# Expert stage: the token sum of a routed row moves from VectorE to POOL, and VectorE finishes the row's targets two steps later

## The reference

```
x = layernorm(x + self_attention(x))
x = layernorm(x + cross_attention(x, ctx))
x = layernorm(x + ffn(x))

ffn: logits = x @ gate_w.T ; the 8 best of 64 experts, their weights by a softmax
     gate, up = split(x @ gu_w[e].T)           # 64 + 64 columns
     out = sum over the 8 experts of weight[e] * ((silu(gate) * up) @ dp_w[e].T)
     out += sigmoid(x @ sh_gate1_w.T) * shared_expert(x)
```

## Time and profile before

| | us |
|---|---|
| median of 3 runs | 1711.96 (1709.74 to 1717.92) |
| the profiled execution | 1717.95 |
| its span, first to last instruction | 1716.2 |
| PE busy, share of the span | 1461.1, 85% |
| DVE busy | 1134.9, 66% |
| POOL busy | 1000.0, 58% |
| ACT busy | 770.8, 45% |
| mean granted TensorE clock | 0.939 |

### The profile page before, as it was taken

One profiled execution on the slowest core, in us unless ns is written; L12 is line 12 of the kernel. 1 busy time (PEld: TensorE's weight loads), 2 busy tenths in 40 slices (PEclk: granted clock), 3 DMA queues, 4 the chain that ended last, 5 costly groups with the idle time before them and its releaser, 6 DMA issues. The chain is left out here.

```text
span 1716.2 us, 35026 instructions
## 1 busy us (share of the span) xinstructions
PE 1461.1 (85%) x9324; PEld 1183.5 (69%) x9324; DVE 1134.9 (66%) x3731; ACT 770.8 (45%) x2649; POOL 1000.0 (58%) x991
## 2 busy tenths in 40 slices
PE   3799999999999999999998727877877787887587
PEld 2688888888888888888887625655655555665464
DVE  2568787878778888888887444455555555344398
ACT  2465656565565565555655112322322232232254
POOL 3446777776766776777766424455555555555322
PEclk8799999999999999999999759899899999889799
DMA  7333232323232212122212946656656556554697
GB/s 259 101 119 104 98 117 83 125 78 119 86 111 75 83 58 80 64 74 66 72 64 83 291 150 186 185 173 174 188 168 186 171 170 177 173 172 134 228 417 318
DMA packets 184341, 247.99 MB, mean 144 GB/s; under 512 B 30796, under 2 KB 160921, under 8 KB 179748
## 3 DMA queue, kind: packets, MB, share of 16 engines
q1 hardware_dynamic: 150820, 171.55, 32.7%
q0 software_dynamic: 27648, 69.28, 11.0%
q10 hardware_dynamic: 5760, 5.87, 1.0%
HBM read 136.98 MB, written 117.98 MB: 149 GB/s over the span
## 5 line engine op out<-in xcount | busy, mean ns | idle before, releaser
L1623 POOL DMA_INDIRECT expert_out_scratch<-y,targets x320 | 318.9, 997 | 277.2 <-DVE targets L1832 104.8
L573 POOL DMA_INDIRECT slot_scratch<-xrow x256 | 273.6, 1069 | 194.4 <-issue 90.4
L1682 PE MATMUL bank_g<-gu,x_turned 128*128 (+1 forms) x1408 | 213.6, 299 | 29.8 <-issue 18.8
L1682 PEld LDWEIGHTS bank_g<-gu,x_turned 128*128 128x128 f32 x1408 | 189.2, 209 | 48.7 <-issue 47.8
L1840 DVE TENSOR_TENSOR inter<-silu,bank_g 128x128 f32<-128x128 f32 x176 | 50.3, 286 | 256.9 <-ACT silu L1748 213.4
L1741 ACT ACTIVATE x_turned<-bank_x 128x512 f32<-128x512 f32 x176 | 105.4, 599 | 231.2 <-PE bank_x L1664 144.7
L860 ACT ACTIVATE q_work<-q_work 128x128 f32<-128x128 f32 x512 | 151.1, 298 | 128.9 <-DVE q_work L1058 110.3
L764 PE MATMUL bank_d<-wo_w,o2t 128*128 128x256 f32 x1536 | 194.5, 287 | 3.0 <-DVE o2t L977 3.0
L764 PEld LDWEIGHTS bank_d<-wo_w,o2t 128*128 128x128 f32 x1536 | 188.7, 194 | 3.1 <-DVE o2t L977 3.1
L1701 PE MATMUL bank_y<-dp,inter_t 64*128 (+1 forms) x352 | 132.8, 460 | 49.7 <-DVE y L1849 23.1
L522 POOL TENSOR_TENSOR q_rs<-q_ve,minus_half 128x8 f32<-128x8 f32 x64 | 105.5, 1648 | 89.4 <-DVE q_ve L1048 88.8
(11 more groups left out here) (253 smaller groups left out, 3225.9 us busy)
## 6 DMA issues: line engine op xcount, KB each, us to landing
x_rows<-slot_scratch SPq DMA_DIRECT2D x320, 136.0 KB
results<-expert_out_scratch SPq DMA_DIRECT2D x32, 1024.0 KB, 8.8
slot_scratch<-zeros SPq DMA_DIRECT2D x16, 816.0 KB, 4.5
dp<-in_down SPq DMA_DIRECT2D x161, 64.0 KB
slot_scratch<-zeros SPq DMA_DIRECT2D x8, 1088.0 KB, 8.4
gu<-in_gate_up SPq DMA_DIRECT2D x11, 768.0 KB
expert_out_scratch<-y,targets POOLq DMA_INDIRECT x320
token_row_scratch<-xrow SPq DMA_DIRECT2D x32, 136.0 KB
```

The costliest lines, as they stand in the source:

```text
L573: nc.gpsimd.indirect_dma_start(out=slot_d[:, :], out_offset=bass.IndirectOffsetOnAxis(ap=xrow[slot][:, SLOT8 + k:SLOT8 + k + 1].bitcast(U3 ...
L1623: nc.gpsimd.indirect_dma_start(out=y_d[:, :], out_offset=bass.IndirectOffsetOnAxis(ap=target[n % 8][:, j:j + 1], axis=0), in_=y[s % HELD][ ...
L1682: mm = nc.tensor.matmul(bank_g[:, s % 2, j * P:(j + 1) * P], xt[s % 2][:, j, c, :], w, start=(c == 0), stop=(c == C - 1))
```

## The change

For every sparse row tile POOL adds `matched` and the token column (`sum_row`, one 128x1 addition per tile, so two per step) into a new tile `summed`. Two rows' sums (n = 0 and 1) are made before the loop. After that `scatter(s)`, behind its three waits, does for j = 0, 1: the sum of tile j of row n + 2, then the indirect DMA of tile j of row n. `matched` and `summed` have 8 places each. DVE's `name_row` is now a maximum with 0 and a minimum with 65535 on `summed`, with the conversion to integer. It runs at s - 2 in the place where it ran at s, that is before `copy_y(s-3)`, and waits for POOL's two sums of its row; `bound_row` too runs at s - 2. `match_row(s)` no longer waits for a name but for the match two rows back, and from row 8 on for POOL's sum 8 rows back. SP's `free_rows` waits for POOL's sum of the row that leaves, not for its name. `find_weights` gets one wait on its own engine's earlier result.

```diff
-        matched = [sb(f"matched{n}", [P, 2]) for n in range(2)]
+        matched = sb("matched", [P, 8, 2])
+        summed = sb("summed", [P, 8, 2])
@@ SP, free_rows
-                        sp.wait_ge(sig["row_named"], number(s - 8) + 1)
+                        sp.wait_ge(sig["row_summed"], 2 * number(s - 8) + 2)
@@ POOL
+            SUMMED_AHEAD = 2
+
+            def sum_row(n, j):
+                if n >= SPARSE_STEPS:
+                    return
+                pool.wait_ge(sig["row_matched"], 2 * n + j + 1)
+                if n >= 8:
+                    pool.wait_ge(sig["row_named"], n - 7)
+                nc.gpsimd.tensor_tensor(summed[:, n % 8, j:j + 1], matched[:, n % 8, j:j + 1],
+                                        x_in[steps_of["sparse", n] % 8][:, j, TOK:TOK + 1], ALU.add)\
+                    .then_inc(sig["row_summed"], 1)
             def scatter(s):
                 n = number(s)
                 pool.wait_ge(sig["y_copied"], s + 1)
                 pool.wait_ge(sig["row_bounded"], n + 1)
                 pool.wait_ge(sig["y_ready"], min(s + 2, STEPS))
                 for j in range(2):
+                    sum_row(n + SUMMED_AHEAD, j)
                     nc.gpsimd.indirect_dma_start(
...
+            for n in range(SUMMED_AHEAD):
+                for j in range(2):
+                    sum_row(n, j)
             for s in range(STEPS):
                 if sparse(s):
                     scatter(s)
@@ DVE, match_row
                 if n >= 2:
-                    dve.wait_ge(sig["row_named"], n - 1)
+                    dve.wait_ge(sig["row_matched"], 2 * n - 2)
+                if n >= 8:
+                    dve.wait_ge(sig["row_summed"], 2 * (n - 7))
...
             def name_row(s):
                 n = number(s)
-                dve.wait_ge(sig["row_matched"], 2 * n + 2)
-                nc.vector.tensor_tensor(named[n % 2][:, :], matched[n % 2][:, :], x_in[s % 8][:, :, TOK], ALU.add)\
+                dve.wait_ge(sig["row_summed"], 2 * (n + 1))
+                nc.vector.tensor_scalar(named[n % 2][:, :], summed[:, n % 8, :], 0.0, 65535.0, ALU.max, ALU.min)\
                     .then_inc(sig["row_named"], 1)
@@ DVE, find_weights
                 if stage == 0:
+                    dve.wait_ge(sig["w_summed"], t)
@@ DVE, order of the loop
-                if now:
-                    name_row(s)
+                named_now = s - 2 >= 0 and s - 2 < STEPS and sparse(s - 2)
+                if named_now:
+                    name_row(s - 2)
                 if 0 <= s - 3 < STEPS:
                     copy_y(s - 3)
-                if now:
-                    bound_row(s)
+                if named_now:
+                    bound_row(s - 2)
```

More of the change, by code:

```diff
@@ L1412 @@
 x_turned x_copied gate_up_done silu_done gated inner_turned inner_copied y_ready y_copied
-row_matched row_named row_bounded
+row_matched row_summed row_named row_bounded
 y_stored0 y_stored1 y_stored2 y_stored3 y_stored4 y_stored5 y_stored6 y_stored7
@@ L1815, in match_row @@
                                                    slot_of[:, 0, 2 * n + j:2 * n + j + 1], column[:, :], ALU.is_equal,
-                                                   ALU.mult, accum_out=matched[n % 2][:, j:j + 1])\
+                                                   ALU.mult, accum_out=matched[:, n % 8, j:j + 1])\
                         .then_inc(sig["row_matched"], 1)
```

## The result

The changed kernel takes 1789.32 us (median, 1782.58 to 1793.89); the kernel before, measured beside it, takes 1714.94. The medians lie 74 us apart (4.3%); the ratio on record, which isn't the one of the medians, is 1.0415, with an interval of 1.0384 to 1.0446. So the change makes the kernel about 4% slower. The forecast was 1798 (1735 to 1885). The profiled execution took 1793.89 us, its span was 1792.2 and the mean granted clock 0.934.

What follows compares the result with a forecast made beforehand. No engine was full; POOL's DMA runs and pauses set 3.31 us a step. With 130 steps at 4.11 us and 46 at 3.0, the stage gains 89 us, less 3 at the end: 1712 + 86 = 1798 us, range 1735 to 1885.

Steps and rivals of the forecast that it cites:

- the ring: Expert stage: projection, POOL's DMA and second sum, DVE's name and copy, next projection wait in a circle; floor 3.72 us.
- tight steps: Expert-stage steps whose name waits for a sum made behind the projection just finished: 130 of 176, at 4.11 us each.
- the first sum: POOL's addition ahead of a scatter's first DMA: adds between 0 and 0.13 us a turn; 0.13 taken.
- lower clock: Projection at 1.2 GHz takes 1.22 us instead of 0.70; in a quarter of the steps, adding 0.13 us a turn.
- The later wake-up: POOL's start after the projection's end: 1.00 us taken instead of 0.87, adding 0.13 us a turn.
- The relaxed steps: Expert-stage steps whose sum is made a scatter earlier: 46 of 176, between 2.23 and 3.31 us, 3.0 taken.
- The end: After the last projection: POOL's last DMA lags 2.3 us instead of 6.2; 3 us taken back.
- the beat of the stage: Expert stage before the change: four POOL DMAs, three gaps and a 2.04 us pause, 6.82 us for two steps.
- the short and the long loop: Expert-stage rivals: all at the 3.72 us floor, 1730 us, chance 0.08; pauses or dearer sums, 1851 to 1919 us, 0.22.
- the main case: Whole kernel: expert stage +89 us, 3 back at its end, 1798 us, own range 1762 to 1840; chance 0.58.
- By POOL's own throughput that costs nothing: POOL's sums in the expert stage: 2 x (1.27 + 0.13) = 2.80 us a step, under the 3.31 of before.
- 64 x 0.68 = 44 us: Sums held up by DVE's 64 two-input weight searches, up to 0.68 us each: 44 us more, 1842 us.

Runs made afterwards that it cites:

- experiment 6: Kernel before, without sums, POOL clearing a small tile between its two DMAs and the copy of y waiting for the clear of two rows earlier: 1729.03 us, 1.1098.
- experiments 1 to 4: Changed kernel with sums one scatter earlier 0.9991, both sums ahead of the first DMA 1.004, name behind copy 0.9969; kernel before plus unread POOL sums 0.9995.
- experiment 5: Changed kernel with every sum made twice, first into a tile that nobody reads: 1809.08 us, 1.1595 against the kernel before on its chip.
- experiment 3: Changed kernel with the name behind the copy of y in DVE's order: 1710.72 us, 0.9969 against the kernel before.
- experiment 9: Kernel before, unchanged, profiled on a chip of the second kind: 1560.99 us, 0.9988.
- experiment 7: Kernel before without the second indirect DMA of every scatter, the last stage reading token rows instead of experts' outputs: 1548.91 us in a single run.
- experiment 4: Kernel before, DVE still adding, naming and bounding as there, plus POOL's 320 sums into a tile that nobody reads: 1713.58 us, 0.9995.
- experiment 11: Kernel before plus POOL's 320 sums into a tile that nobody reads, on a chip of the second kind: 1603.24 us, 1.03.
- experiment 8: Changed kernel with sums made one scatter earlier and the name behind the copy, on a chip of the second kind: 1588.19 us, 1.0189.

## Why the prediction was right, by its own steps

**The mechanism** was right, and it is shown and not only argued: closing the ring without any sum loses the time (experiment 6, on a chip of the second kind), opening it at any of three places, or leaving out the wait, gives it back (experiments 1 to 4, on the first chip).

**The ring's terms**, by the medians of the tight steps of the changed kernel:

| term | forecast | measured |
|---|---|---|
| projection's end to the first DMA, with the first sum | 0.87 + 0.13 + 0.13 | 0.94 (0.94 to 1.38) |
| the DMA | 0.97 | 1.00 |
| second sum and handing over | 0.13 + 0.05 | 0.22 + 0.04 |
| name, until the copy starts | 0.07 | 0.08 |
| copy | 0.69 | 0.69 |
| copy's end to the projection's end | 0.24 + 0.70 | 0.94 |
| lower clock | 0.13 | none in the median, at most 0.08 in the mean |
| **a turn** | **4.11** | **3.92** (mean 4.02) |

- *The sum* was mis-sized: 0.206 us in the mean, not 0.13. The way I got 0.13, extrapolating two wide additions to width 1, gives over a third too little; it lay inside the bounds of 0.13 and 0.65.
- *The first sum* costs nearly nothing: POOL starts it 0.24 us after the projection's end (1107.38 - 1107.14), and there are 0.52 us of gap behind it. A DMA of an idle POOL took 0.87 us to start without a sum and 0.94 with one: most of the sum lies inside the start-up (with two sums ahead of the DMA it is 0.98, experiment 5). I had added it whole.
- *The later wake-up* of 0.13 was not needed; the mean is 0.96, with the first sum in it, and the worst 1.38.
- *The clock.* I wrote "under 0.92 in the stage", at PE 55% busy. It was 0.92 and 0.95, at 73% and 71% busy by the rows above, no lower than in the earlier trace rows. The error is in the 2.23 of 4.1: that is PE's shortest turn, but PE is busy 0.73 x 3.71 = 2.7 us a step here, and was 0.80 x 3.31 = 2.6 before. The mean of the tight steps stands 0.10 over the median: 0.08 lie between the copy's end and the projection's end, where the projection takes up to 1.22 us instead of 0.70, and 0.02 in late wake-ups.
- *The relaxed steps*: 3.0 forecast, 2.81 in the mean of 42 (median 2.49).
- *Number of steps*: by the projections' ends, without the first ten, the tight ones went from 3.20 to 4.02 us (123 of them: +101 us) and the relaxed ones from 3.69 to 2.81 (42: -37). The two together make 64 of the 70 us; the first ten make up the rest. The stage's forecast was +89 and it became +70, by terms that were nearly all a little too large.
- *The end*: I took 3 us back, it was 1.2. POOL's last DMA starts 4.7 us behind the last projection's end in the changed kernel, not 2.3: the last two rows, four DMAs and not two, are still scattered one after another behind it. (Before it was 5.95 us and not 6.2, as the last projection ran at the lower clock and took 0.63 us, not 0.38.)
- *What the sum didn't have*: the stage begins 7 us later. The start of the first projection differs by up to 17 us among the profiled kernels (1019.2 in experiment 6, 1036.2 in experiment 3), in no order that I can tie to an edit. Why is open.

**Some of it was luck.** The errors of the ring partly cancel: wake-up and first sum 0.19 us too dear, the second sum with its handing over 0.08 too cheap, the clock 0.05 too dear. The price of the relaxed steps stood on an explanation of the pauses that failed (below). And only the first chip made the size of the change right: on the second kind the changed kernel's 1774 us still lie in the range that I gave, but the change costs 213 us there and not the 86 that I forecast.

**The signs that I named** came: the wait before the name, the sums between the DMAs, hardly a run of four, no sum under a DMA. Two didn't: the clock (above), and PE's wait for the copy, which is 57.2 us and not "well over 100", because somewhat more (67.8) is booked as "issue" in front of the same instruction. The two together are 125.

**A step that failed** is the explanation of the pace before, although the sum didn't suffer from it. I read the pauses of 2.04 us as what follows a run of four POOL DMAs and called 6.82 us for two steps the beat of the stage. The 32 pauses of the earlier trace rows alone can't be that beat: in 560 us they are one in 17.5 us, not one in 6.82. (All of POOL's gaps over 1.6 us in the stage, whatever they are put down to, are 71, and 48 of them follow a run of four.) On another chip 276 of these DMAs run back to back without one pause (experiment 9). So a run of four isn't enough to make them; they belong to the first chip, or to something on it that the trace doesn't show. Their cause is open: experiment 7 was meant to tell, and ran where there was nothing to tell. What the runs do show is that where they exist, a ring that idles POOL makes them vanish nearly all (5.6 us instead of 60.2 on ACT's silu) and the relaxed steps are 37 us shorter; that the one brought the other is likely but not tested. The forecast of the short and the long loop hung on this; the main case took over only its price for the relaxed steps.

**"By POOL's own throughput that costs nothing"** is right on the first chip (experiment 4: 0.9995) and wrong on the others (experiment 11: 1.03), where a step took 2.37 us before and POOL's row takes 2 x 1.27 = 2.54. I compared 2.80 with 3.31, a pace in which PE itself lost 1.1 us a step. Compared with the 2.23 us of the earlier trace rows, the cost would have been seen: 160 x 2.54 = 406 us of scatters alone fill the 415 us of the stage in experiment 9.

**The weight search and the sums.** I gave the rule of the Trainium skill (SBUF — State Buffer, Who interferes with whom) only a place among the ways to a longer loop, since DVE waits idle when the second sum runs. The trace bears out both. In the changed kernel only 4 sums behind 1040 us took over 0.3 us, 0.53 to 0.76, some 2 us together, so there was nearly nothing of the 64 x 0.68 = 44 us that I had set beside the forecast; but each of the 4 lay under a two-input search, as did all 14 of experiment 11. The same holds for the indirect DMAs, as in the earlier trace rows: 20 of experiment 9 and 8 of the changed kernel took over 1.1 us, and every one started during such a search and ended 0.84 to 0.88 us behind it. The rule says that a DVE instruction with two SBUF inputs contends with a GpSimd instruction that reads SBUF, for an exclusive lock, and that one with at most one SBUF input, outside DVE's 2-port modes, doesn't. The sums of experiment 11 agree on either half.

**No better version.** The name behind the copy is 0.3% faster than the kernel before on the first chip (0.9969, hardly clear of noise) and 3.2% slower on the second kind (1.032). On a chip without pauses every version with POOL's sums lost, by 1.9% at the least (experiment 8).

## What to carry to other kernels

Before work is handed to another engine ahead of time, follow the chain once round: when the thing handed over stands behind an item that itself waits for your own latest result, "two steps ahead" is a ring, and its length in that order, not the size of the work, is the new step. One step more of distance, or the waiting instruction behind the one that others need, opens it. And price a busy engine's new work against the pace that the stage would have without its unexplained pauses, not against the pace that one trace shows.

## What the runs showed of the hardware

- The same kernel takes 1716 us on one chip and 1560 on three others. The difference is in the expert stage (3.31 us a step against 2.37), with instructions of the same median length (the projection's 480 ns, POOL's indirect DMA 0.97 us); on the slower one ACT and POOL stand still for some 2 us at a time with a releaser that the profile doesn't know.
- An idle POOL starts an indirect DMA 0.87 us after the projection that it waited for; a 128x1 addition of the same POOL runs at 0.24 us, and the DMA then starts at 0.94. So by these start times, which the profile gives only roughly on POOL, most of the delay is the DMA's own start and not POOL's waking.
- Small additions on POOL overlap: 0.18 to 0.21 us long, 0.14 apart (experiment 5). Behind a sum the gap to the next DMA is 0.16 us, where between two DMAs it is 0.30, so two sums lengthen POOL's row by 0.22 us and not by their 0.42.
